# One VectorE instruction over real and imaginary part, for the rotations and the closing products of a convolution, in a transformer layer with experts

## The chip, the cores and the metric

The kernel runs on one core of a Trainium2 chip. The metric is device time of one execution in microseconds. The number given for a kernel is the median of its runs. Profiles come from one execution each. TensorE multiplies matrices, VectorE and ScalarE work on elements, GpSimd works on elements and issues indirect transfers, and SyncE issues the plain ones. In the rows of the profile they are PE, DVE, ACT, POOL and SP. Each engine takes its own instructions strictly in order and waits for the others at semaphores.

## What is computed

The input x has 8 batches of 1024 positions with 128 channels, in float32. The reference, cut to what matters:

```python
# block 1, on h = layernorm(x) without parameters
h = layernorm(h, gamma, beta)
conv = ifft(fft(filt) * fft(h))            # filt[t] = phazor**t * phazor_init
h = real(conv + last_conv * prog * phazor) # prog[t] = phazor**t
x1 = h + xn                                # xn = layernorm(x)
x = x + x1 + (silu(layernorm(x1) @ w1 + b1) @ w2 + b2)
# block 2: 8 experts, the best 2 of each token, weighted by a softmax over the two
x = x + moe(layernorm(x))
```

The kernel does the convolution without a Fourier transform, as a recurrence along the positions, for each of the 128 channels. With channels on the partitions, u (the normalized input, 128 x 1024) is multiplied by a complex table `in`. Real part `vr` and imaginary part `vi` are each scanned along the 1024 positions with a real decay. Then both are multiplied by a table `out`, and the result is the difference of the two products.

## The kernel before

Work is staged by batch. TensorE turns a batch's normalized rows so that channels lie on partitions (`hn_turn`), ScalarE copies the turned rows out as u (`conv_input`), VectorE does the convolution, TensorE turns it back (`conv_turn`), and VectorE adds it to xn (`x1_sum`, line 1189) and takes mean and variance (`moments`). GpSimd makes scale and shift out of these (`x1_scales`, lines 557 to 560), ScalarE normalizes with them (`x1_norm`, line 661), TensorE turns the rows (`h2_turn`), multiplies up (`mlp_up`) and down (`mlp_down`) with a SiLU of ScalarE between. VectorE adds the residual (`x2_sum`), the moments go through GpSimd and ScalarE again (`x2_scales`, `x2_norm`), and the rows are routed. For each batch VectorE chooses the pair of experts (`choose`) and computes each row's place (`positions`), and GpSimd scatters the batch's eight tiles of 128 rows to device memory by indirect transfers (`sort_rows`, line 584). When six batches are sorted, the experts begin on tiles of rows, which takes the last 200 us.

The input's own statistics run further ahead: VectorE's `x_statistics` and `x_moments`, then GpSimd's `x0_scales` (lines 546 to 551, with a power at line 549), then ScalarE's two normalizations (`x0_norm`, line 674, and `x0_plain_norm`, line 681).

The order on each engine is written out by hand. Round i handles several batches at once: on VectorE the residual sum of batch i - 1, `x1_sum` of i + 1, the choice of i - 2, the input's statistics of i + 4, the rotations of i + 2, the moments of i + 4, the positions of i - 2, and the scans, products and subtraction of i + 2. Batches 0 and 1 come before the rounds, and there the scans follow the rotations at once. On GpSimd a round does `x2_scales`, `x1_scales`, an accumulating transfer of x1 (`add_x1`), `x0_scales` of batch i + 3, and the eight scatters of batch i - 2.

All tensors of the convolution are slots of one buffer `work` of 128 x 18 x 1024 floats: in_re and in_im are slots 0 and 1, out_re and out_im slots 2 and 3, u is slot 6, vr and vi slots 7 and 8. For each of the eight batches VectorE runs seven instructions of 1024 columns: `vr = u * in_re` (line 1210), `vi = u * in_im` (1215), a scan of vr (1221) and of vi (1223), `vr = vr * out_re` (1224), `vi = vi * out_im` (1226) and `vi = vr - vi` (1231). An instruction that uses the result of the one in front of it waits for a semaphore that this one raises. `s_vo` orders VectorE's own work through `then` and `mark`; `s_ui` says that both rotations are done (ScalarE may write the next u), `s_vi` that vi is scanned, `s_ti` that vi is multiplied, `s_conv` that the convolution is ready.

Of the kernel before, what the change touches and what calls it, by code (L numbers as in the profile page):

```python
# [4 lines left out]
BATCHES, LENGTH, D = 8, 1024, 128  # L5
# [62 lines left out]
def block_moe_kernel(nc, x, cols, w1, w2, b2, router, mw1, mw2, out):  # L68
# [5 lines left out]
    ALU = mybir.AluOpType  # L74
# [7 lines left out]
    with ctx, nc.allow_low_precision(reason="counts of at most 64 are whole in bf16"):  # L82
        def sb(name, shape, dt=f32):
            return ctx.enter_context(nc.sbuf_tensor(name, shape, dt))

        def sem(name):
            return ctx.enter_context(nc.semaphore(name))
# [17 lines left out]
        work = sb("work", [128, 18, LENGTH])  # L105

        def slot(k):
            return work[:, k, :]

        def tiled(ap):  # L110
            return ap.rearrange("p (j d) -> p j d", d=D)

        in_re, in_im, out_re, out_im = slot(0), slot(1), slot(2), slot(3)
        hn, xn = tiled(slot(4)), tiled(slot(5))
        u, vr, vi = slot(6), slot(7), slot(8)
        x1, h2 = [tiled(slot(9)), tiled(slot(13))], tiled(slot(10))
# [16 lines left out]
        start_v = sb("start_v", [128, 4])  # L133
# [159 lines left out]
        s_vo = sem("vector_order")  # L293
# [6 lines left out]
        s_ui = sem("u_im_ready")  # L300
        s_vi = sem("v_im_ready")
        s_ti = sem("out_im_ready")
        s_conv = sem("conv_ready")
        s_t2 = sem("conv_turned")
# [49 lines left out]
        def after(eng, semaphore, count):  # L354

            if count > 0:
                eng.wait_ge(semaphore, count)
# [16 lines left out]
        def live(b):  # L374
            return 0 <= b <= LAST
# [740 lines left out]
        def _(v):  # L1116
            d = nc.vector
# [10 lines left out]
            def mark(ins):  # L1128

                ins.then_inc(s_vo, 1)  # L1130
                ordered[0] += 1
                return ordered[0]

            def then(ins):
                v.wait_ge(s_vo, mark(ins))
# [35 lines left out]
            def x2_sum(b):  # L1171
                v.wait_ge(s_dn, (b + 1) * FC)
                v.wait_ge(s_res[b], 16)
                if live(b - ROWBUFS):
                    v.wait_ge(s_sort[b - ROWBUFS], 16 * TPB)
                d.tensor_tensor(x2_of(b), tiled(down_p[:, :]), batch_of(resid, b), ALU.add).then_inc(s_x2, 1)

            def x2_stats(b):
                v.wait_ge(s_x2, b + 1)
                after(v, s_sc2, b)  # L1180
                moments(lambda j: x2_of(b)[:, j, :], stats2, mom2, s_x2m)
# [21 lines left out]
                after(v, s_sc0, b - 1)  # L1203
                aggregates(stats0, mom0[b % 2], s_x0m)

            def rotate_re(b):

                v.wait_ge(s_u, b + 1)
                after(v, s_conv, b)
                return mark(d.tensor_tensor(vr, u, in_re, ALU.mult))  # L1210

            def rotate_im(b):

                after(v, s_t2, b)
                d.tensor_tensor(vi, u, in_im, ALU.mult).then_inc(s_ui, 1)

            def scans(b, rotated):

                decay = decay_factor.to_broadcast([128, LENGTH])
                v.wait_ge(s_vo, rotated)  # L1220
                then(d.tensor_tensor_scan(vr, decay, vr, start_v[:, 0:1], ALU.mult, ALU.add))
                v.wait_ge(s_ui, b + 1)
                d.tensor_tensor_scan(vi, decay, vi, start_v[:, 1:2], ALU.mult, ALU.add).then_inc(s_vi, 1)
                then(d.tensor_tensor(vr, vr, out_re, ALU.mult))
                v.wait_ge(s_vi, b + 1)
                d.tensor_tensor(vi, vi, out_im, ALU.mult).then_inc(s_ti, 1)

            def convolution(b):

# [47 lines left out]
            def choose(b):  # L1277

                choose_first(b)
                choose_others(b)  # L1280
                choose_second(b)
                choose_pair(b)
                choose_places(b)
# [79 lines left out]
            def iteration(i):  # L1363


                b0, b1, b2, b4, chosen_b = i - 1, i + 1, i + 2, i + 4, i - 2
                if live(b0):
                    x2_sum(b0)
                if live(b0):
                    x2_stats(b0)  # L1370
                if live(b1):
                    x1_sum(b1)
                if live(chosen_b):
                    choose(chosen_b)
                if live(b4):
                    counted = x_statistics(b4)
                if live(b2):
                    rotated = rotate_re(b2)
                    rotate_im(b2)
                if live(b4):  # L1380
                    x_moments(b4, counted)
                if live(chosen_b):
                    positions(chosen_b)
                if live(b2):
                    scans(b2, rotated)
                if live(b2):
                    convolution(b2)

# [102 lines left out]
            tables(first_moments)  # L1491
            v.wait_ge(s_decay, 1)
            v.wait_ge(s_tab, 1)
            rotated = rotate_re(0)
            rotate_im(0)
            scans(0, rotated)
            convolution(0)
            weights()
            x1_sum(0)
            x_moments(2, x_statistics(2))  # L1500
            rotated = rotate_re(1)
            rotate_im(1)
            scans(1, rotated)
            convolution(1)
            x_moments(3, x_statistics(3))
            iteration(0)
# [121 lines left out]
```

## Time and profile before

| | us |
|---|---|
| median of 3 runs | 444.3 |
| lowest and highest run | 443.93, 446.59 |
| the profiled execution's own time | 446.09 |
| its span, first to last instruction | 444.3 |
| VectorE busy in the span | 349.3 (79%) |
| TensorE busy | 376.9 (85%) |
| ScalarE busy | 319.5 (72%) |
| GpSimd busy | 271.5 (61%) |

The profiled execution took 1.8 us more than its span, which lies around the instructions. In the rows of a timeline the first number is the start in us from the span's beginning and the second how long the instruction (or a run of like ones) lasted; a bracket behind it is the idle time of its engine in front of it and the instruction that ended it. An instruction's row can reach a little into the next one's, since it is counted until its last result is written; the distance from start to start is what it occupies of the engine.

### The profile page before, as it was taken

To read this page: it belongs to the slowest core of one execution; us is meant where nothing else is said; L and a number is where in the kernel's file an instruction comes from. 1 tells how busy PE (TensorE), PEld (TensorE's weight loads), DVE (VectorE), ACT (ScalarE), POOL (GpSimd) and SP (SyncE) were. 2 spreads that over 40 slices of the span, in tenths; PEclk is the share of its full clock that TensorE was granted. 3 is DMA by queue.
4 is the path that set the end of the run, shared out by engine and by line. 5 is a ranking of instruction groups with operands and counts; after the bars stand their busy time and mean duration, and the time that the engine had idled before them with its cause. 6 is when DMAs were issued, how large, how long until landed. Compare 5 with 4: busy or idle time off the path is not lost.

```text
span 444.3 us, 11234 instructions
## 1 busy us (share of the span) xinstructions
PE 376.9 (85%) x2723; PEld 321.1 (72%) x2723; DVE 349.3 (79%) x1332; ACT 319.5 (72%) x772; POOL 271.5 (61%) x339
## 2 busy tenths in 40 slices
PE   1173288797999999989979899999999999999970
PEld 1131257484867768666748899899999999999970
DVE  7999999798899989897652777887677777777770
ACT  4792586978889798689544786677777777777740
POOL 6890955645687798756483376477654555545451
PEclk9996589998989898999997999999999999999995
DMA  7649222110222221231323243444433333333200
GB/s 247 188 144 321 83 49 48 29 20 14 48 89 47 89 62 50 70 93 51 90 86 115 59 143 113 120 147 131 115 92 94 104 102 102 107 100 109 70 3 0
DMA packets 34434, 41.60 MB, mean 94 GB/s; under 512 B 5382, under 2 KB 29459, under 8 KB 34244
## 3 DMA queue, kind: packets, MB, share of 16 engines
q1 hardware_dynamic: 27236, 23.56, 18.4%
q0 software_dynamic: 7136, 17.33, 13.5%
q8 instruction: 25, 0.41, 0.4%
q14 instruction: 37, 0.30, 0.2%
HBM read 19.52 MB, written 18.92 MB: 86 GB/s over the span
## 4 chain that ended last, share of the span: by engine, by line
PE 55%; POOL 13%; DVE 11%; ACT 6%; issue 6%; POOLq 0%; DVEq 0%; ACTq 0%
PE up_p L1057 12%; PE down_p L1076 12%; PE down_p L876 8%; POOL sorted_rows L584 6%; PE turn_p L1057 5%; PE turn_p L1076 5%; PE up_p L865 5%; PE turn_p L853 3%; PE up_p L1066 2%; ACT work L674 2%; POOL scale L549 2%; PE route_p L918 2%; DVE stats L1158 1%; ACT rows L688 1%; ACT work L681 1%
## 5 line engine op out<-in xcount | busy, mean ns | idle before, releaser
L620 POOL DMA_INDIRECT out<-result,out_id x91 | 89.4, 983 | 68.1 <-DVE result L1564 47.2
L584 POOL DMA_INDIRECT sorted_rows<-rows,pos x64 | 71.8, 1122 | 37.6 <-issue 27.2
L865 PE MATMUL up_p<-h_t,work 128*128 128x512 f32 x128 | 67.7, 653 | 9.4 <-ACT work L648 8.1
L1057 PE MATMUL up_p<-xt,work 128*128 128x128 f32 x520 | 69.4, 277 | 0.6 <-ACT hid_t L806 0.5
L876 PEld LDWEIGHTS down_p<-w_sb,work 128*128 128x128 f32 x512 | 62.2, 196 | 9.9 <-issue 9.3
L1076 PE MATMUL down_p<-mw_sb,hid_t 128*128 x520 | 69.1, 276 | 0.1
L821 ACT ACTIVATE work<-mw_c 128x256 f32 x182 | 65.8, 416 | 0.3 <-issue 0.2
L876 PE MATMUL down_p<-w_sb,work 128*128 128x128 f32 x512 | 64.5, 281 | 0.1
L1057 PEld LDWEIGHTS up_p<-xt,work 128*128 128x128 f32 x520 | 63.2, 192 | 1.2 <-issue 1.1
L1076 PEld LDWEIGHTS down_p<-mw_sb,hid_t 128*128 128x128 f32 x520 | 63.3, 192 | 0.6 <-issue 0.5
L806 ACT ACTIVATE hid_t<-up_p 128x512 f32<-128x512 f32 x65 | 38.8, 597 | 29.8 <-PE up_p L1057 29.6
L853 PE MATMUL turn_p<-ident,work 128*128 128x128 f32 x192 | 29.9, 308 | 27.2 <-ACT work L674 11.4
L853 PEld LDWEIGHTS turn_p<-ident,work 128*128 128x128 f32 x192 | 25.6, 161 | 35.0 <-ACT work L674 11.5
L865 PEld LDWEIGHTS up_p<-h_t,work 128*128 128x128 f32 x128 | 23.8, 208 | 33.9 <-issue 19.0
L648 ACT ACTIVATE work<-up_p,b_all 128x512 f32<-128x512 f32 x64 | 40.5, 675 | 10.1 <-PE up_p L865 9.7
L1558 DVE SCALAR_TENSOR_TENSOR biased<-down_p,tin,biased 128x128 f32<-128x128 f32 x65 | 22.8, 350 | 23.6 <-PE down_p L1076 22.0
L1540 DVE SCALAR_TENSOR_TENSOR biased<-b_all,tin 128x128 f32<-128x128 f32 x91 | 32.0, 352 | 9.7 <-issue 9.7
L661 ACT ACTIVATE work<-work,shift,scale 128x128 f32<-128x128 f32 x64 | 25.5, 480 | 16.4 <-POOL shift L560 16.4
L1547 DVE SCALAR_TENSOR_TENSOR biased<-b_all,tin,biased 128x128 f32<-128x128 f32 x91 | 32.0, 352 | 3.6 <-issue 1.5
L801 ACT ACTIVATE xt<-up_p,one_col 128x128 f32<-128x128 f32 x91 | 33.0, 362 | 1.0 <-PE up_p L1066 1.0
L688 ACT ACTIVATE rows<-rows,shift,scale 128x128 f32<-128x128 f32 x64 | 25.5, 481 | 4.7 <-POOL shift L575 4.7
L549 POOL TENSOR_TENSOR scale<-var_eps,neg_half 128x16 f32<-128x16 f32 x8 | 27.2, 3405 | 0.7
(248 smaller groups left out, 744.2 us busy)
## 6 DMA issues: line engine op xcount, KB each, us to landing
tin<-sorted_rows SPq DMA_DIRECT2D x91, 136.0 KB, 2.2
resid<-in_x SPq DMA_DIRECT2D x8, 512.0 KB, 3.8
resid<-work POOLq DMA_DIRECT2D x8, 512.0 KB, 4.7
sorted_rows<-zeros SPq DMA_DIRECT2D x29, 136.0 KB, 2.4
out<-result,out_id POOLq DMA_INDIRECT x91, 2.3
work<-in_mw SPq DMA_DIRECT2D x1, 1024.0 KB, 6.3
sorted_rows<-rows,pos POOLq DMA_INDIRECT x64, 2.5
work<-in_w SPq DMA_DIRECT2D x1, 256.0 KB
```

The lines of the kernel that those rows point to most:

```text
L549: then(g.tensor_tensor(scale0[b % 2][:, :, :].rearrange("p a b -> p (a b)"), var_eps[:, :, :].rearrange("p a b -> p (a b)"), neg_half[:, : ...
L584: g.indirect_dma_start(sorted_dram, bass.IndirectOffsetOnAxis(pos[b % 2][:, j:j + 1], 0), rows[b % ROWBUFS][:, j, :], None).then_inc(s_sor ...
L620: g.indirect_dma_start(out_rows, bass.IndirectOffsetOnAxis(out_id[k][:, :], 0), result[k][:, :], None, bounds_check=TOKENS - 1, oob_is_err ...
L648: s_.activation(half(silu[c % 2], h), up_p[k % 3][:, :], ACT.Silu, bias=b1_all[:, c:c + 1])\
L801: s_.activation(xt[s % DEEP][:, :], xt_p, ACT.Identity, bias=one_col[:, :]).then_inc(s_xs, 1)
L806: s_.activation(hid_t[s % DEEP][:, :], mid_banks[bank_of(s)][:, :], ACT.Gelu).then_inc(s_gelu, 1)
L821: last = s_.activation(ring[s % RING][:, k * EF:(k + 1) * EF], mw1_c[:, bass.ds(at[k], EF)], ACT.Copy)
L853: last = t.transpose(turn_p[:, j * TILE:(j + 1) * TILE], src(j), ident[:, :])
L865: t.matmul(dst, w1_g[:, k], half(h_t, h), start=True, stop=True).then_inc(s_up, 1)
L876: last = t.matmul(down_p[:, j * D:(j + 1) * D], silu[c % 2][:, j * TILE:(j + 1) * TILE], w2_sb[:, c, :], start=False, stop=c == FC - 1, sk ...
L1057: last = t.matmul(mid_banks[bank_of(s)][:, c * TILE:(c + 1) * TILE], ring[s % RING][:, c * 128:(c + 1) * 128], xt[s % DEEP][:, :], start=T ...
L1076: last = t.matmul(y_banks[bank_of(s)][:, e * D:(e + 1) * D], hid_t[s % DEEP][:, c * 128:(c + 1) * 128], mw2_sb[:, bass.ds(at, D)], start=c ...
```

## The change

The two rotations become one instruction of 2 x 1024 columns. It reads u for both parts (the same 1024 columns twice), in_re with in_im, and writes vr with vi, which lie in neighbouring slots. The two products by `out` become one in the same manner. The scans stay two instructions, as does the subtraction. The order marks between the parts (`s_vo`) go: the first scan waits for `s_ui`, the fused product for `s_vi`. The fused rotation waits for the turned convolution of the batch before (`s_t2`) as a whole; only the imaginary part's rotation did so before.

```diff
+        both_in, both_out, both_v = work[:, 0:2, :], work[:, 2:4, :], work[:, 7:9, :]
...
-            def rotate_re(b):
+            def rotate(b):
 
                 v.wait_ge(s_u, b + 1)
                 after(v, s_conv, b)
-                return mark(d.tensor_tensor(vr, u, in_re, ALU.mult))
-
-            def rotate_im(b):
-
                 after(v, s_t2, b)
-                d.tensor_tensor(vi, u, in_im, ALU.mult).then_inc(s_ui, 1)
-
-            def scans(b, rotated):
+                d.tensor_tensor(both_v, u.unsqueeze(1).to_broadcast([128, 2, LENGTH]), both_in, ALU.mult).then_inc(s_ui, 1)
+
+            def scans(b):
 
                 decay = decay_factor.to_broadcast([128, LENGTH])
-                v.wait_ge(s_vo, rotated)
-                then(d.tensor_tensor_scan(vr, decay, vr, start_v[:, 0:1], ALU.mult, ALU.add))
                 v.wait_ge(s_ui, b + 1)
+                d.tensor_tensor_scan(vr, decay, vr, start_v[:, 0:1], ALU.mult, ALU.add)
                 d.tensor_tensor_scan(vi, decay, vi, start_v[:, 1:2], ALU.mult, ALU.add).then_inc(s_vi, 1)
-                then(d.tensor_tensor(vr, vr, out_re, ALU.mult))
                 v.wait_ge(s_vi, b + 1)
-                d.tensor_tensor(vi, vi, out_im, ALU.mult).then_inc(s_ti, 1)
+                d.tensor_tensor(both_v, both_v, both_out, ALU.mult).then_inc(s_ti, 1)
```

The calls follow: `rotate(b)` stands where `rotate_re(b)` and `rotate_im(b)` stood, and `scans(b)` takes no count.

VectorE's instructions around the rotations and scans of batch 2, before; `x0_scales`, `vector_order` and the like are semaphores, `work` is the buffer of all slots:

```order
L1210 TENSOR_TENSOR work<-work 128x1024 [waits conv_ready,u_ready]
L1215 TENSOR_TENSOR work<-work 128x1024 [waits conv_turned]
L1152 MEMSET spare_v 128x1 [waits x0_scales,vector_order]
L1164 BN_AGGR mom<-stats 128x2 x8
L1221 SCALAR_TENSOR_TENSOR work<-mag,start_v,work 128x1024 [waits vector_order]
L1223 SCALAR_TENSOR_TENSOR work<-mag,start_v,work 128x1024 [waits u_im_ready,vector_order]
L1224 TENSOR_TENSOR work<-work 128x1024
L1226 TENSOR_TENSOR work<-work 128x1024 [waits v_im_ready,vector_order]
L1231 TENSOR_TENSOR work<-work 128x1024 [waits out_im_ready]
```

The same place in the changed kernel, whose lines are numbered anew (1218 and 1219 are the scans, 1226 the subtraction):

```order
L1212 TENSOR_TENSOR work<-work 128x2048 [waits conv_turned,conv_ready,u_ready]
L1153 MEMSET spare_v 128x1 [waits x0_scales,vector_order]
L1165 BN_AGGR mom<-stats 128x2 x8
L1218 SCALAR_TENSOR_TENSOR work<-mag,start_v,work 128x1024 [waits u_im_ready]
L1219 SCALAR_TENSOR_TENSOR work<-mag,start_v,work 128x1024
L1221 TENSOR_TENSOR work<-work 128x2048 [waits v_im_ready]
L1226 TENSOR_TENSOR work<-work 128x1024 [waits out_im_ready]
```

Nothing changes places: seven instructions of 1024 columns become five, two of them with 2048. The wait between the two scans is gone, and the one in front of the products has moved ahead of both of them. The other engines' instructions are the same.

## Rows read from the trace of the kernel before

**Rows 1.** the chain that ended last, share of the span by engine (page, part 4)

```profile
PE 55%; POOL 13%; DVE 11%; ACT 6%; issue 6%; POOLq 0%; DVEq 0%; ACTq 0%
```

**Rows 2.** VectorE in order of time around batch 1: start us, us, engine, line

```profile
46.57 1.19 DVE L1210 TENSOR_TENSOR work<-work 128x1024 f32<-128x1024 f32 x1
47.68 1.23 DVE L1215 TENSOR_TENSOR work<-work 128x1024 f32<-128x1024 f32 x1
48.83 2.34 DVE L1221 TENSOR_TENSOR_SCAN work<-mag,start_v,work 128x1024 f32<-128x1024 f32 x1
51.20 2.36 DVE L1223 TENSOR_TENSOR_SCAN work<-mag,start_v,work 128x1024 f32<-128x1024 f32 x1
53.49 1.20 DVE L1224 TENSOR_TENSOR work<-work 128x1024 f32<-128x1024 f32 x1
54.72 1.23 DVE L1226 TENSOR_TENSOR work<-work 128x1024 f32<-128x1024 f32 x1
55.98 1.23 DVE L1231 TENSOR_TENSOR work<-work 128x1024 f32<-128x1024 f32 x1
```

**Rows 3.** groups by line: busy us, mean ns of one, idle before

```profile
L1246 DVE TENSOR_TENSOR first<-scored,pick 128x64 f32<-128x64 f32 x8 | 1.8, 225 | 0.3
```

**Rows 4.** GpSimd in order of time, the same stretch

```profile
44.50 0.20 POOL L557 TENSOR_TENSOR tmp<-mom,neg_one 128x8 f32<-128x8 f32 x1 [10.94 <-DVE mom L1164]
...
46.67 1.16 POOL L560 TENSOR_TENSOR shift<-tmp,scale 128x8 f32<-128x8 f32 x1
47.79 1.17 POOL L546 TENSOR_TENSOR var_eps<-mom,eps 128x8 f32<-128x8 f32 x1
48.93 2.24 POOL L547 TENSOR_TENSOR tmp<-mom,neg_one 128x8 f32<-128x8 f32 x1
51.23 0.20 POOL L548 TENSOR_SCALAR var_eps<-mom 128x8 f32<-128x8 f32 x1
51.51 4.75 POOL L549 TENSOR_TENSOR scale<-var_eps,neg_half 128x16 f32<-128x16 f32 x1
56.34 0.94 POOL L551 TENSOR_TENSOR shift<-tmp,scale 128x16 f32<-128x16 f32 x1
```

**Rows 5.** durations of two GpSimd lines: ns min/median/max, first to last start

```profile
L549 POOL TENSOR_TENSOR scale<-var_eps,neg_half x8: 2920/2936/4903, 14.1 to 163.8; 128x16 f32<-128x16 f32 x8
...
L584 POOL DMA_INDIRECT sorted_rows<-rows,pos x64: 956/965/3115, 117.8 to 294.7; - x64
```

**Rows 6.** ScalarE in order of time, the same stretch

```profile
47.86 3.18 ACT L661 ACTIVATE work<-work,shift,scale 128x128 f32<-128x128 f32 x8 [10.34 <-POOL shift L560]
...
57.31 3.19 ACT L674 ACTIVATE work<-resid,shift,scale 128x128 f32<-128x128 f32 x8
```

**Rows 7.** VectorE, then GpSimd, then ScalarE around batch 7's rotations

```profile
184.97 1.22 DVE L1210 TENSOR_TENSOR work<-work 128x1024 f32<-128x1024 f32 x1
186.11 1.22 DVE L1215 TENSOR_TENSOR work<-work 128x1024 f32<-128x1024 f32 x1
...
185.85 0.40 POOL L560 TENSOR_TENSOR shift<-tmp,scale 128x8 f32<-128x8 f32 x1
...
186.28 3.18 ACT L661 ACTIVATE work<-work,shift,scale 128x128 f32<-128x128 f32 x8 [3.24 <-POOL shift L560]
```

**Rows 8.** VectorE, then GpSimd, then ScalarE, batches 5 and 6

```profile
138.34 1.21 DVE L1210 TENSOR_TENSOR work<-work 128x1024 f32<-128x1024 f32 x1
...
147.81 1.22 DVE L1226 TENSOR_TENSOR work<-work 128x1024 f32<-128x1024 f32 x1
...
137.40 2.92 POOL L549 TENSOR_TENSOR scale<-var_eps,neg_half 128x16 f32<-128x16 f32 x1
...
145.50 1.93 POOL L584 DMA_INDIRECT sorted_rows<-rows,pos  x1 [0.30 <-issue]
147.73 0.96 POOL L584 DMA_INDIRECT sorted_rows<-rows,pos  x1 [0.30 <-issue]
...
159.78 3.19 ACT L661 ACTIVATE work<-work,shift,scale 128x128 f32<-128x128 f32 x8 [0.79 <-POOL shift L560]
```

More of the change, by code:

```diff
@@ L1377, in iteration @@
                 if live(b2):
-                    rotated = rotate_re(b2)
-                    rotate_im(b2)
+                    rotate(b2)
                 if live(b4):
@@ L1384, in iteration @@
                 if live(b2):
-                    scans(b2, rotated)
+                    scans(b2)
                 if live(b2):
@@ L1493, in _ @@
             v.wait_ge(s_tab, 1)
-            rotated = rotate_re(0)
-            rotate_im(0)
-            scans(0, rotated)
+            rotate(0)
+            scans(0)
             convolution(0)
@@ L1500, in _ @@
             x_moments(2, x_statistics(2))
-            rotated = rotate_re(1)
-            rotate_im(1)
-            scans(1, rotated)
+            rotate(1)
+            scans(1)
             convolution(1)
```

## The prediction

> **What bounds the kernel now.** I read the chain of waits that ended last first: TensorE holds 55% of it, GpSimd 13, VectorE 11, ScalarE 6 [rows 1]. All eight fused pairs lie in the first 200 of 444.3 us, where the chain passes from engine to engine, so I read that stretch in order of time, engine by engine. Around batch 1 VectorE never rests: rotation, rotation, scan, scan, product, product, subtraction start one behind the other from 46.57 to 55.98 us [rows 2]. Beside it GpSimd works out the scales of the next normalizations. Such an instruction of 8 columns takes 0.20 us when it meets no long VectorE instruction (44.50), but 1.16, 1.17 and 2.24 us at 46.67, 47.79 and 48.93, and each of these ends 0.12 to 0.15 us behind the start of the next VectorE instruction: 47.83 against 47.68, 48.96 against 48.83. The power at line 549 takes 4.75 us here and 2.92 at least [rows 2, 4, 5]. So a GpSimd instruction that begins while VectorE reads two SBUF operands lasts until that VectorE instruction is over. ScalarE waits for the outcome: 10.34 us for line 560, and its normalization at 57.31 starts 0.03 us behind the end of line 551 at 57.28 [rows 4, 6]. That wait, GpSimd behind VectorE and ScalarE behind GpSimd, is what the change touches.
>
> In the Trainium skill, "SBUF — State Buffer", section "Who interferes with whom", has this as a rule: a VectorE instruction with two SBUF inputs and a GpSimd instruction that reads SBUF exclude each other, and the later one stands still for the whole of the other. The stretched lines above agree with it. By that rule the two GpSimd terms below hold; without it only the VectorE gains would be left.
>
> **The change part by part.** *The fused instruction.* No row shows one of 2048 columns. Two products of the same kind: 64 columns take 0.225 us [rows 3], 1024 take 1.19 to 1.23 [rows 2], which is (1.21 - 0.225) / 960 = 1.03 ns a column; so 2048 take 1.21 + 1024 x 0.00103 = 2.26 us. From start to start an instruction that waits for nothing occupies 1.11 to 1.15 us (46.57 to 47.68, 47.68 to 48.83), and one whose successor needs its result 1.23 to 1.26 (53.49 to 54.72 to 55.98), some 0.1 more. The fused one then occupies 2.20, or 2.30 before a successor that needs it. From below the bound is 2 x (1.21 - 0.225) = 1.97 (nothing but columns), from above 2 x 1.26 = 2.52 (nothing saved). I take 2.20 and 2.30, the straight line through the rows.
>
> *VectorE, per batch.* The rotations took 2.26 together; 2.20 now where statistics stand between them and the scans (six batches), 2.30 where the scan follows at once (batches 0 and 1). From the first scan to the subtraction 7.15 us pass now (48.83 to 55.98): 2.37, 2.29, 1.23, 1.26. The wait between the scans goes (2.29 in place of 2.37), the second scan gets one before the fused product (2.37 for 2.29), and the pair costs 2.30 for 2.49: 6.96. So a batch gains 0.15 to 0.25 us, some 1.8 us of VectorE's time over eight batches. Most of it is not on the chain: VectorE waits for TensorE or ScalarE later in the same round. On the chain I count batch 0's, 0.1 us. The added wait for the turned convolution before the real part costs nothing: the residual sum that stands ahead of it on VectorE has waited for the same turn, and in batch 0 nothing is waited for.
>
> *Beside batch 1's rotations and products.* Line 560 (for batch 0's residual sum) starts 0.10 us behind the rotation (46.67, 46.57). Its end moves from 47.83 to 46.57 + 2.20 + 0.15 = 48.92, and ScalarE's normalization at 47.86 moves by 1.09 [rows 2, 4, 6]. Then line 546, line 547 and line 548 each need a turn. Before, they had the seams at 48.83 and 51.20, and the power began inside the second scan: 51.51, released when the product started at 53.49, and 2.77 us later, at 56.26, done. After, the seams are 48.87 (rotation to scan), 51.16 and 53.53 (scan to product). With the first one spent on line 560, at most line 546 slips through; line 547 stands behind the first scan and line 548 behind the second or on the seam. The power starts inside the fused product and is released at 53.53 + 2.20 = 55.73: done at 58.5, line 551 at 58.8 instead of 57.28. That is +1.5 for the normalization at 57.31. The least it can be is 0 (GpSimd finds a place at the middle of the fused instructions); 1.1 stands by line 560 alone.
>
> *Beside batch 7's rotations, line 560 again* (for batch 6's residual sum). It starts at 185.85 inside the first rotation (184.97), is done at 186.25, 0.14 behind the start of the second at 186.11, and ScalarE, which had waited 3.24 us, starts at 186.28 [rows 7]. The fused rotation starts 0.16 earlier by batch 6's shorter scans and products, and ends at 184.81 + 2.20 = 187.01: line 560 at 187.15, +0.9. Bounds: 0, and 1.1 without the earlier start. Beside the other batches' rotations line 560 was not held so long, and I count nothing there.
>
> *Sum.* -0.1 + 1.5 + 0.9 = +2.3 us. The profiled execution took 446.09 us (span 444.3), so it would take 448.4. The median before is 444.3, 1.8 below that execution; the same sum on it gives 446.6.
>
> **The rivals.** *GpSimd is not held longer, and the time falls.* Place: line 560 beside the rotations of batches 1 and 7. If a waiting read gets in between the two halves of the fused instruction, the port is free after some 1.1 us as before, and both GpSimd terms are 0. What is left are the gains on the chain: 0.1 in batch 0, 0.16 for scans and product of batch 4 and 0.07 for batch 5's rotation: -0.3, 444.0. If every gain of 1.8 counted it would be 442.5. It decides from the point where line 560 beside batch 1 lasts about 1.2 us and not 2.2. For it: no row shows an instruction of two halves. Against it: nothing in the rows shows a read let in before an instruction's end, and a scan of 2.34 us held line 547 for 2.24.
>
> *More is lost, in the sorting.* The row scatters of line 584 take 0.965 us in the median, but 1.93 at 145.50, behind a scan. The third, at 147.73, takes 0.96: it began 0.08 us before the second product of its batch (147.81), on the seam between the products [rows 5, 8]. That seam is gone, so a third scatter should stand behind the fused product, +1.0 us. For batch 4's scans this makes GpSimd later in front of batch 5: the power at 137.40 ran free, and would start at about 138.4, behind the rotation at 138.34 that now lasts until 140.4; it would end at 143.3 instead of 140.32, and after what GpSimd then waited for VectorE anyway about 2.0 us are left at the end of the next eight scatters. The scales behind them hold ScalarE at 159.78 (0.79 us of waiting). If all of it passes on: 2.3 + 2.0 = +4.3, 448.6. Against it: it is a race of some 0.1 us, and the next scan waits for TensorE, which gives GpSimd time to catch up. The same section of the Trainium skill says that descriptor generation should not be held by a product, as it needs the write side only; by that this rival would add nothing. The 1.93 and 3.1 us of line 584 under the scans speak against it.
>
> *The fused instruction does not run at one column per 1.03 ns,* with one operand read twice over. At 2.52 the rotation and the product of batch 1 and the rotation of batch 7 each hold GpSimd 0.3 longer: 446.6 + 0.9 = 447.5.
>
> **How the numbers follow.** Forecast, slower by about 2.3: 0.52, with its own range 445.2 (the 0.9 beside batch 7 alone) to 447.5 (the upper price of the instruction). Not held: 0.27, 442.5 to 444.8. More lost: 0.18. Slow instruction: 0.03. The range is 443.2 to 449.2: it leaves out the lower half of the second case and what the third may add beyond its sum. One per cent, 4.4 us, is about what a measurement of this kernel tells from no change. Slower by more takes the third case, nearly half of it (0.08), and 0.02 of the forecast's tail: 0.10. Faster by more than 4.4 is beyond all the gains of 1.8 together: 0.02. Within 1%: 0.88.
>
> **What would show it.** Right: fused instructions of about 2.26 us; line 560 beside batch 1's rotation over 2 us, and the normalization at 47.86 a microsecond later against that rotation; line 551 there after the subtraction's end; line 560 beside batch 7's rotation about 1.1 to 1.3 us; three of eight scatters stretched under batches 4 and 5 in place of two. Wrong: line 560 at 1.2 us or less, the normalizations at 57.31 and 186.28 no later, or an end that moves although they do not.

## The result and the profile after

The changed kernel takes 454.24 us in the median of 6 runs (451.92 to 458.29). Beside them the kernel before took 446.63 us (443.93 to 447.65, 6 runs). The ratio is 1.0179, with a 95% interval of 1.0125 to 1.0233: slower by 7.6 us, where I had forecast 2.3 and a range that ended at 449.2. The profiled execution took 452.99 us, with a span of 451.2.

In the profile the lines below the diff are numbered anew: the rotation is line 1212, the scans 1218 and 1219, the product 1221, the subtraction 1226. All lines of GpSimd and ScalarE are one higher: 561 is before's 560, 550 the power, 585 the scatters, 662 and 675 the normalizations.

The chain that ended last, by engine, answers to [rows 1]:

```profile
PE 57%; ACT 11%; POOL 10%; DVE 7%; issue 6%; DVEq 0%; POOLq 0%; ACTq 0%
```

ScalarE's share grew from 6 to 11%, and VectorE's, whose instructions became fewer, fell from 11 to 7. The chain now passes more often through ScalarE's normalizations; the shares alone do not show what they waited for, so the rows in order of time have to.

VectorE around batch 1, in order of time (start us, us), answers to [rows 2]:

```profile
46.21 2.26 DVE L1212 TENSOR_TENSOR work<-work 128x2048 f32<-128x2048 f32 x1
48.50 2.35 DVE L1218 TENSOR_TENSOR_SCAN work<-mag,start_v,work 128x1024 f32<-128x1024 f32 x1
50.77 2.33 DVE L1219 TENSOR_TENSOR_SCAN work<-mag,start_v,work 128x1024 f32<-128x1024 f32 x1
53.13 2.29 DVE L1221 TENSOR_TENSOR work<-work 128x2048 f32<-128x2048 f32 x1
55.46 1.23 DVE L1226 TENSOR_TENSOR work<-work 128x1024 f32<-128x1024 f32 x1
```

The fused instruction takes 2.26 to 2.29 us, as computed, and from the first instruction to the subtraction 9.25 us pass instead of 9.41. GpSimd in the same stretch, to [rows 4]:

```profile
46.31 2.22 POOL L561 TENSOR_TENSOR shift<-tmp,scale 128x8 f32<-128x8 f32 x1
48.49 0.19 POOL L547 TENSOR_TENSOR var_eps<-mom,eps 128x8 f32<-128x8 f32 x1
48.65 2.20 POOL L548 TENSOR_TENSOR tmp<-mom,neg_one 128x8 f32<-128x8 f32 x1
50.92 2.17 POOL L549 TENSOR_SCALAR var_eps<-mom 128x8 f32<-128x8 f32 x1
53.17 5.01 POOL L550 TENSOR_TENSOR scale<-var_eps,neg_half 128x16 f32<-128x16 f32 x1
58.26 0.22 POOL L552 TENSOR_TENSOR shift<-tmp,scale 128x16 f32<-128x16 f32 x1
```

Line 561 lasts 2.22 us for 1.16, to the end of the fused rotation. The next instruction slips through on the seam at 48.50, the two behind it stand one behind each scan, and the power is held by the fused product and done at 58.18. That is 11.97 us behind the start of the rotation, where the prediction had 11.93 (58.5 against 46.57). ScalarE's two normalizations, to [rows 6]:

```profile
48.56 3.18 ACT L662 ACTIVATE work<-work,shift,scale 128x128 f32<-128x128 f32 x8 [12.12 <-POOL shift L561]
...
58.51 3.19 ACT L675 ACTIVATE work<-resid,shift,scale 128x128 f32<-128x128 f32 x8 [0.61 <-POOL shift L552]
```

The second starts 1.2 us later than before (57.31). Counted from the start of the rotation, which itself came 0.36 earlier, the first is 1.06 us later than before and the second 1.56, as forecast (1.09 and 1.5). What the forecast did not count comes seventy microseconds later. The sorting of batch 0 beside batch 4's scans and products in the kernel before (GpSimd, then VectorE, then the normalization that follows on ScalarE):

```profile
121.06 1.92 POOL L584 DMA_INDIRECT sorted_rows<-rows,pos  x1 [0.30 <-issue]
123.28 0.96 POOL L584 DMA_INDIRECT sorted_rows<-rows,pos  x1 [0.30 <-issue]
...
123.34 1.22 DVE L1226 TENSOR_TENSOR work<-work 128x1024 f32<-128x1024 f32 x1
...
135.34 3.19 ACT L661 ACTIVATE work<-work,shift,scale 128x128 f32<-128x128 f32 x8 [0.41 <-POOL shift L560]
```

and in the changed kernel, with the two places further on where fused rotations meet GpSimd (batch 5's at 140.22, batch 6's at 162.94); this answers to [rows 8]:

```profile
123.13 1.78 POOL L585 DMA_INDIRECT sorted_rows<-rows,pos  x1 [0.30 <-issue]
125.21 2.06 POOL L585 DMA_INDIRECT sorted_rows<-rows,pos  x1 [0.30 <-issue]
...
140.41 4.87 POOL L550 TENSOR_TENSOR scale<-var_eps,neg_half 128x16 f32<-128x16 f32 x1
...
163.80 1.49 POOL L561 TENSOR_TENSOR shift<-tmp,scale 128x8 f32<-128x8 f32 x1
...
177.04 2.09 POOL L585 DMA_INDIRECT sorted_rows<-rows,pos  x1 [0.30 <-issue]
...
204.28 2.08 POOL L585 DMA_INDIRECT sorted_rows<-rows,pos  x1 [0.30 <-issue]
...
124.16 2.29 DVE L1221 TENSOR_TENSOR work<-work 128x2048 f32<-128x2048 f32 x1
126.48 1.22 DVE L1226 TENSOR_TENSOR work<-work 128x1024 f32<-128x1024 f32 x1
...
140.22 2.27 DVE L1212 TENSOR_TENSOR work<-work 128x2048 f32<-128x2048 f32 x1
...
162.94 2.29 DVE L1212 TENSOR_TENSOR work<-work 128x2048 f32<-128x2048 f32 x1
...
138.38 3.18 ACT L662 ACTIVATE work<-work,shift,scale 128x128 f32<-128x128 f32 x8 [1.37 <-POOL shift L561]
...
165.32 3.18 ACT L662 ACTIVATE work<-work,shift,scale 128x128 f32<-128x128 f32 x8 [2.80 <-POOL shift L561]
```

The third scatter, which used the seam between the two products (123.28 against 123.34), now begins inside the fused one and lasts to 127.27, 0.79 us beyond the start of the subtraction at 126.48: 2.06 us for 0.96. So are the third scatters of batches 2 and 3, at 177.04 (2.09) and 204.28 (2.08), which took 0.96 and 0.97 before. Then the power begins 0.19 us behind batch 5's fused rotation and takes 4.87 us for 2.92. Line 561 in front of batch 5's normalization takes 1.49 us for 0.20. ScalarE's waits for line 561 grow with it: 0.41 to 1.37, 0.79 to 2.80.

The Trainium skill, "SBUF — State Buffer", section "Who interferes with whom", infers that descriptor generation is not held by such a product, as it needs the write side. Here the scatter beside the fused product took 2.06 us and its five successors 0.96, so for these indirect transfers the measurement decides otherwise.

Beside batch 7's rotation nothing was held, against the forecast [rows 7]:

```profile
189.99 0.20 POOL L561 TENSOR_TENSOR shift<-tmp,scale 128x8 f32<-128x8 f32 x1
...
190.50 2.29 DVE L1212 TENSOR_TENSOR work<-work 128x2048 f32<-128x2048 f32 x1
```

GpSimd, late by some 4 us, now comes 0.5 us before the rotation there and no longer inside it. The ranges of the two lines of [rows 5] and of line 561 (ns min/median/max) sum up who is held: the power's median rises from 2936 to 3432, the scatters' stays, and the longest of line 561 takes 2223 where line 560 had 1157.

```profile
L550 POOL TENSOR_TENSOR scale<-var_eps,neg_half x8: 2921/3432/5009, 13.8 to 167.0; 128x16 f32<-128x16 f32 x8
...
L585 POOL DMA_INDIRECT sorted_rows<-rows,pos x64: 956/965/2981, 119.9 to 301.2; - x64
...
L561 POOL TENSOR_TENSOR shift<-tmp,scale x8: 201/202/2223, 46.3 to 217.3; 128x8 f32<-128x8 f32 x8
```

### The profile page after: what moved, and what is told of

Read it like the earlier page. It is cut to its first block, busy times and chain, and to the rows that moved or that the text cites. A ratio compares the mean times of both kernels' runs of the same rounds, so it can differ in the third digit from the quotient of the medians.

```text
span 451.2 us, 11202 instructions
## 1 busy us (share of the span) xinstructions
PE 377.5 (84%) x2723; PEld 322.0 (71%) x2723; DVE 347.7 (77%) x1316; ACT 319.3 (71%) x772; POOL 288.1 (64%) x339
## 4 chain that ended last, share of the span: by engine, by line
PE 57%; ACT 11%; POOL 10%; DVE 7%; issue 6%; DVEq 0%; POOLq 0%; ACTq 0%
PE up_p L1058 12%; PE down_p L1077 12%; PE down_p L877 9%; POOL sorted_rows L585 6%; PE turn_p L1058 5%; PE up_p L866 5%; PE turn_p L1077 5%; PE turn_p L854 4%; ACT work L662 3%; ACT work L675 3%; ACT work L682 2%; PE up_p L1067 2%; ACT rows L689 2%; ACT work L649 1%; PE route_p L919 1%
## 5 line engine op out<-in xcount | busy, mean ns | idle before, releaser
L585 POOL DMA_INDIRECT sorted_rows<-rows,pos x64 | 76.7, 1198 | 41.0 <-issue 23.2
L866 PE MATMUL up_p<-h_t,work 128*128 128x512 f32 x128 | 65.4, 632 | 16.3 <-ACT work L649 15.1
L877 PEld LDWEIGHTS down_p<-w_sb,work 128*128 128x128 f32 x512 | 63.8, 200 | 10.5 <-issue 9.9
L877 PE MATMUL down_p<-w_sb,work 128*128 128x128 f32 x512 | 66.3, 286 | 0.1
L550 POOL TENSOR_TENSOR scale<-var_eps,neg_half 128x16 f32<-128x16 f32 x8 | 30.5, 3811 | 0.7
```

The lines of the kernel that those rows point to most:

```text
L585: g.indirect_dma_start(sorted_dram, bass.IndirectOffsetOnAxis(pos[b % 2][:, j:j + 1], 0), rows[b % ROWBUFS][:, j, :], None).then_inc(s_sor ...
L866: t.matmul(dst, w1_g[:, k], half(h_t, h), start=True, stop=True).then_inc(s_up, 1)
L877: last = t.matmul(down_p[:, j * D:(j + 1) * D], silu[c % 2][:, j * TILE:(j + 1) * TILE], w2_sb[:, c, :], start=False, stop=c == FC - 1, sk ...
```

## The experiments

Ratios are against the kernel before, run beside them. Two theories stood against each other at first. *Length*: an instruction twice as long holds GpSimd twice as long. *Seams*: what was lost are the waits and places between instructions that the change also removed or moved.

**The change in parts.** Four kernels: the rotations fused alone (second scan and products as before, their own waits kept); the products fused alone; both fused over the parts, but over 512 columns at a time, so that there are as many instructions as before; and nothing fused with the changed kernel's waits.

```diff
# e2_product_only, against the changed kernel
-                d.tensor_tensor(both_v, u.unsqueeze(1).to_broadcast([128, 2, LENGTH]), both_in, ALU.mult).then_inc(s_ui, 1)
+                d.tensor_tensor(vr, u, in_re, ALU.mult)
+                d.tensor_tensor(vi, u, in_im, ALU.mult).then_inc(s_ui, 1)
# e4_waits_only: the same, and
-                d.tensor_tensor(both_v, both_v, both_out, ALU.mult).then_inc(s_ti, 1)
+                d.tensor_tensor(vr, vr, out_re, ALU.mult)
+                d.tensor_tensor(vi, vi, out_im, ALU.mult).then_inc(s_ti, 1)
# e1_rotation_only, against the changed kernel
-                d.tensor_tensor_scan(vr, decay, vr, start_v[:, 0:1], ALU.mult, ALU.add)
+                then(d.tensor_tensor_scan(vr, decay, vr, start_v[:, 0:1], ALU.mult, ALU.add))
...
+                then(d.tensor_tensor(vr, vr, out_re, ALU.mult))
                 v.wait_ge(s_vi, b + 1)
-                d.tensor_tensor(both_v, both_v, both_out, ALU.mult).then_inc(s_ti, 1)
+                d.tensor_tensor(vi, vi, out_im, ALU.mult).then_inc(s_ti, 1)
# e3_halves_of_columns, against the changed kernel (the rotation in the same way)
-                d.tensor_tensor(both_v, both_v, both_out, ALU.mult).then_inc(s_ti, 1)
+                for h in range(2):
+                    last = d.tensor_tensor(halves(both_v, h), halves(both_v, h), halves(both_out, h), ALU.mult)
+                last.then_inc(s_ti, 1)
```

e1, rotations alone:

> Only the two rotations are one instruction; scans and products with their waits are those of before. Length theory (GpSimd's reads are held for as long as the VectorE instruction with two SBUF operands lasts, and 2.29 us holds longer than 1.2): line 560 beside batches 1, 2 and 6 stays held (1.5 to 2.2 us each), the third scatter of each batch is free again (0.96 us); about 449 to 451 us against 446.6 before and 454.2 changed. Seam theory (the loss comes from the waits that went, which left gaps for GpSimd): the scans and products have their waits, so about the time of before, 446 to 448.

Measured: 448.53 us, ratio 1.0059 (1.002 to 1.0099): a small loss, just below what *length* expected and just above *seams*.

e2, products alone:

> Only the two products are one instruction, and the scans follow each other without a wait; the rotations are two. Length theory: line 560 of batch 1 lasts 1.2 us as before, the third scatter of batches 4 to 7 is held (about 2 us), the power in front of batch 5's scatters races with the rotation; 448 to 451 us. If it is the rotation alone that costs: 446 to 447.

Measured: 453.22 us, ratio 1.0143 (1.0057 to 1.0229), more than was expected.

e3, both in halves of the columns:

> Both parts in one instruction, but of 2 x 512 columns, two of them for the rotation and two for the product: as many instructions of 1024 columns as before, with the operand shapes and the waits of the changed kernel. Length theory: no GpSimd instruction is held over 1.2 us by them, line 560 beside batch 1 lasts about 1.2 us; 445 to 448 us. Rival (the form of the operands, u read twice, or the waits that went are what costs): 452 to 455.

Measured: 446.31 us, ratio 0.9995 (0.9951 to 1.004), as *length* expected.

e4, the waits alone:

> Nothing is fused; only the waits are those of the changed kernel (no wait between the scans or between the products). Length theory: line 560 as before, VectorE 0.1 to 0.2 us per batch shorter; the third scatter can lose the gap between the products, which costs up to 1.1 us a batch; 445 to 449 us. Seam theory: most of the loss, 451 to 455.

Measured: 446.57 us, ratio 1.0001 (0.9963 to 1.0039), as *length* expected.

The same columns and operands, paired in the same way, cost nothing when each instruction stays at 1.2 us, and the waits cost nothing either. The length is the cause. The products weigh more than the rotations (1.4% and 0.6%), though the forecast had most of its loss at a place where both meet GpSimd. The third scatter shows what the product's length does: it takes 2.07 us beside the fused product and 1.00 beside the halves. GpSimd of e2, then of e3:

```profile
124.31 2.07 POOL L585 DMA_INDIRECT sorted_rows<-rows,pos  x1 [0.30 <-issue]
```

```profile
124.04 1.00 POOL L585 DMA_INDIRECT sorted_rows<-rows,pos  x1 [0.30 <-issue]
```

**Out of the rotation's way.** In e5 the changed kernel's rotation waits until the scales of the batch before are made, so that it cannot hold line 561. In e6 the product is in halves besides, as in e3.

```diff
                 after(v, s_t2, b)
+                after(v, s_sc1, b)
```

> The changed kernel, and the fused rotation waits until GpSimd has the scale and shift of x1 of the batch before (line 560 of the kernel before). Length theory: line 560 lasts 0.20 us beside every batch, ScalarE's normalizations of x1 beside batches 1, 2 and 6 are no longer late by it, VectorE gives up to 1 us of its own waiting; what the product costs stays: 450 to 453 us. If the rotation cost nothing beyond the product: 454 as the changed kernel.

Measured: 452.01 us, ratio 1.0147 (1.0075 to 1.0219). Line 561 takes 0.20 us everywhere, and 1.5% stay.

> As e5_wait_for_scales, and the product over both parts comes in two instructions of 2 x 512 columns. Length theory: both held reads are gone, the third scatter of a batch lasts about 1 us: 444 to 447 us, at or a little below the kernel before. Rival (more than held reads is lost): 449 or more.

Measured: 448.1 us, ratio 1.001 (0.9959 to 1.0061): the time lies between the two expectations, the ratio is not separable from 1. With the product halved, what is left of the change costs nothing that can be measured: a fused rotation behind line 561 is free, and the 1.5% of e5 are the product's.

**Shorter still.** If length costs, shorter scans should gain. e7 is e3 with each scan in two of 512 columns, the second one starting from the last column of the first.

```diff
-                d.tensor_tensor_scan(vr, decay, vr, start_v[:, 0:1], ALU.mult, ALU.add)
-                d.tensor_tensor_scan(vi, decay, vi, start_v[:, 1:2], ALU.mult, ALU.add).then_inc(s_vi, 1)
-                v.wait_ge(s_vi, b + 1)
+                for h in range(2):
+                    for k, part_of in ((0, vr), (1, vi)):
+                        first = start_v[:, k:k + 1] if h == 0 else part_of[:, HALF - 1:HALF]
...
+                v.wait_ge(s_vi, 4 * b + 4)
```

> As e3_halves_of_columns, and the two scans in halves of 512 columns too, the second half of each going on from the last column of the first: no VectorE instruction of the convolution is over about 1.3 us. Length theory carried on: the first two scatters of a batch last about 1.9 and 1.0 us instead of 2.9 and 1.9, the power at line 549 less than 4.2; VectorE pays 0.1 to 0.4 us a batch; 441 to 445 us, below both kernels. Rival (the held reads of the scans are not on the path): 446 to 449.

Measured: 448.63 us, ratio 1.0044 (1.0004 to 1.0084): slower, where a gain was expected. The held instructions did become shorter, the first scatter of batch 0 from 2.91 to 1.84 us and two powers from 4.75 and 4.90 to 3.79 and 3.83. Others became longer: a third power went from 2.92 to 3.98, the third scatter of batch 2 from 0.96 to 1.96, and the scans take 2.45 and 2.43 us a pair of halves, for 2.34 in one. That the time follows from these is argued; no run takes them apart.

**TensorE's clock.** In the changed profile the granted clock is at the lower level (1.2 of 2.4 GHz) for most of two stretches of rounds 4 and 5, behind waits of TensorE of 2.64 and 2.33 us for ScalarE (us, busy times of the engines, clock as a share of full speed, DMA share, GB/s; before has 1.00 in both). Over the whole profile the mean is not lower, 0.949 against 0.942 before.

```profile
158.00:166.00 8.00, 7.63 (x29) 6.10 (x30) 6.74 (x28) 4.04 (x7) 7.58 (x11) 0.58 0.10 35
186.00:193.00 7.00, 7.00 (x28) 5.59 (x27) 6.34 (x26) 5.36 (x12) 4.95 (x7) 0.54 0.21 50
```

e8 is the changed kernel with eight unused matmuls in those waits.

```diff
+                    if b in (4, 5) and c == 1 and h == 1:
+                        pe.wait_ge(s_x2, b)
+                        for _ in range(8):
+                            t.matmul(down_p[:, 0:128], ones_f[:, :], mean_f[:, :], start=True, stop=True)
                     after(pe, s_silu, n - 2)
```

> The changed kernel with eight matmuls of 128 columns, whose result is not used, in the two waits of TensorE (2.64 and 2.33 us) behind which it ran at half clock in rounds 4 and 5. If the half clock is part of the loss: granted clock near 1.0 from 158 to 166 and from 186 to 193 us of the span, eight matmul pairs of the down projection in 2.0 us and not 3.8, and the time 2 to 4 us below the changed kernel, 450 to 452. If it is beside the path: 453 to 455.

Measured: 454.55 us, ratio 1.0206 (1.0131 to 1.0281). The clock stayed at full in both stretches, and fell elsewhere:

```profile
80.00:105.00 25.00, 22.01 (x121) 16.78 (x119) 18.87 (x59) 19.28 (x42) 12.69 (x14) 0.86 0.11 22
158.00:166.00 8.00, 7.14 (x43) 5.15 (x42) 7.47 (x37) 5.00 (x9) 7.06 (x11) 1.00 0.16 54
186.00:193.00 7.00, 6.14 (x33) 4.18 (x33) 6.51 (x29) 6.74 (x14) 4.69 (x7) 1.00 0.21 42
225.00:240.00 15.00, 15.00 (x80) 11.32 (x79) 8.68 (x45) 4.38 (x9) 10.42 (x13) 0.84 0.24 85
```

Keeping the clock full at these two places gave none of the 2 to 4 us. That does not put the clock off the path. In the changed kernel's chain the down projection (line 877) of the first stretch takes twice as long as the next one, start and us:

```profile
162.42 3.71 PE down_p L877 x16
...
167.91 1.78 PE down_p L877 x16
```

Where e8 gained by this and lost it again is shown behind the table below.

**Which batches.** e9, e10 and e12 keep the rotations apart, with the changed kernel's waits, and fuse the products in batches 4 to 7 (scatters run beside them), in 0 to 3 (none do), and in 4 and 5.

```diff
+                if b >= 4:
+                    d.tensor_tensor(both_v, both_v, both_out, ALU.mult).then_inc(s_ti, 1)
+                else:
+                    d.tensor_tensor(vr, vr, out_re, ALU.mult)
+                    d.tensor_tensor(vi, vi, out_im, ALU.mult).then_inc(s_ti, 1)
# e10: if b < 4, e12: if b in (4, 5)
```

> Separate rotations with the changed kernel's waits; the two products are fused in batches 4 to 7 only, where row scatters run beside them. Theory that the loss comes from the scatters (third scatter held by the fused product, GpSimd late for the next scales): most of what the fused products cost everywhere comes back, 450.5 to 454 against a kernel before at 446.5; third scatter of the first batch sorted about 2.06 us, line 560's instruction beside batch 2 about 0.5. Rival, the prediction's own place (the scales beside batch 1, before any scatter): under 1 us is lost, 446 to 448.

Measured: 452.73 us, ratio 1.0156 (1.0087 to 1.0226), as the theory of the scatters expected.

> The same with the products fused in batches 0 to 3 only, where no row scatter runs. Theory of the scatters: 445.5 to 447.5, third scatters 0.96 us. Rival, the scales of the early batches (power 4.9 us beside batch 1, then 3.9 at 74.5 beside batch 2): 450 to 453, and the normalizations of x1 later by a microsecond or more from the third one on.

Measured: 448.86 us beside 447.8 for the kernel before, ratio 1.0019 (0.9978 to 1.0061). By the ratio nothing measurable is lost.

> Separate rotations with the changed kernel's waits; the products are fused in batches 4 and 5 only (fused in 4 to 7 they cost 1.56%). If the loss is a sum of single delays, here it is that of one third scatter (+1.1 us) and of the power behind it (+0.9 us): ratio 1.003 to 1.007, third scatter of the first sorted batch about 2.06 us, of the three others about 0.96. If instead only the last rounds before the experts count (what comes earlier is made up again while other engines wait): ratio 0.997 to 1.002. If the first delay sets all that follows late: 1.010 or more.

Measured: 451.57 us, ratio 1.0089 (1.0052 to 1.0126), between two of the expectations: more than the sum of the delays that the rows show. In its profile they are one third scatter (2.07 for 0.96 us) and one power (3.80 for 2.92). The rows do not explain the 0.89%, as the table below shows.

The place is settled by e9 and e10: what the products measurably cost, they cost beside the scatters. The size is not: some 2 us of held instructions in e12 beside 4.0 us of time.

**The delay by itself.** e13 and e14 take the kernel before, with nothing fused, and let GpSimd's fourth scatter wait until the subtraction beside it is done; e13 does so for batches 0, 2 and 3, e14 for batch 0.

```diff
                 for j in tiles:
+                    if b in (0, 2, 3) and j == 3:
+                        pool.wait_ge(s_conv, b + 5)
                     g.indirect_dma_start(sorted_dram, bass.IndirectOffsetOnAxis(pos[b % 2][:, j:j + 1], 0),
```

> The kernel before, nothing fused; GpSimd's fourth scatter of batches 0, 2 and 3 waits until VectorE's subtraction beside it is done, which starts it some 1.3 us later than before (third scatters stay at 0.96 us). Theory that a late GpSimd is the whole cause and that its lateness costs more than itself: 5 to 9 us, ratio 1.011 to 1.020, as the fused products of batches 4 to 7 cost. If each delay passes on one to one: three times 1.3 and up to 1.0 at a power, ratio 1.006 to 1.011. If the fused product does something else besides: under 1.005.

Measured: 454.06 us, ratio 1.0184 (1.014 to 1.0229), as the first theory expected.

> The same wait for batch 0's fourth scatter only. One to one: 1.3 us, and up to 1.0 at the power behind it, ratio 1.003 to 1.006. If the lateness costs more than itself, as in the kernel with fused products in batches 4 and 5: 1.006 to 1.012. If something else in the fused product costs the time: 0.998 to 1.002.

Measured: 453.2 us, ratio 1.0167 (1.0125 to 1.0209), above every expectation. GpSimd, then ScalarE, of e14:

```profile
127.70 0.96 POOL L586 DMA_INDIRECT sorted_rows<-rows,pos  x1 [1.86 <-DVE work L1233]
...
139.69 1.52 POOL L547 TENSOR_TENSOR tmp<-mom,neg_one 128x8 f32<-128x8 f32 x1
141.29 1.07 POOL L548 TENSOR_SCALAR var_eps<-mom 128x8 f32<-128x8 f32 x1
142.44 2.92 POOL L549 TENSOR_TENSOR scale<-var_eps,neg_half 128x16 f32<-128x16 f32 x1
...
138.57 3.19 ACT L663 ACTIVATE work<-work,shift,scale 128x128 f32<-128x128 f32 x8 [2.03 <-POOL shift L560]
```

One wait lets GpSimd stand 1.86 us instead of 0.30, 1.56 more, at one place of the kernel before, and the kernel loses 1.67%, some 7 us (5.6 to 9.3 by the interval), about what the change loses. What two more such waits add, the runs do not separate from nothing. A late GpSimd is enough for a loss of this size; a fused product need do nothing else.

How it grows can be followed when each profile is counted from its own first `placed` (VectorE's instruction that computes the rows' places, line 1288 before, 1283 after), which puts aside what differs earlier in an execution. Times are in us behind it:

| | before | waits only (e4) | changed | changed, waits filled (e8) | products of 4, 5 (e12) | one delay (e14) |
|---|---|---|---|---|---|---|
| `placed` of batch 0 in the profile | 116.67 | 118.22 | 118.74 | 120.39 | 121.28 | 118.26 |
| batch 0 sorted, GpSimd goes on | 13.92 | 13.83 | 14.88 | 14.87 | 14.89 | 15.48 |
| ScalarE's `x1_norm` behind it | 18.67 | 18.57 | 19.64 | 19.64 | 19.65 | 20.31 |
| first scatter of batch 1 | 25.63 | 25.52 | 27.52 | 27.52 | 27.61 | 27.97 |
| the next `x1_norm` | 43.11 | 42.92 | 46.58 | 46.59 | 45.63 | 45.99 |
| `placed` of batch 2 | 48.10 | 48.10 | 51.84 | 48.65 | 48.66 | 52.50 |
| the experts' first upward product | 131.36 | 131.75 | 136.26 | 136.33 | 132.52 | 136.24 |
| mean granted clock in between | 0.94 | 0.95 | 0.95 | 0.96 | 0.97 | 0.92 |

From that product on all six take about the same time to the end of their spans (195.8 to 196.4 us). Against the kernel with the waits alone, the changed one is 1.05 late when batch 0 is sorted, which is the held third scatter, 2.0 at the next scatters, which adds the held power, 3.7 at the next normalization, in front of which line 561 is held, and 4.5 when the experts begin. e14 goes the same way.

Behind the next scatters two things mix. One is collisions: GpSimd's instructions, now later, come to lie inside the next rotations and are held again (lines 547 and 548 in e14, the power in the changed kernel), and ScalarE waits 1.4 to 2.8 us where it waited 0.4 to 0.8. The other is TensorE's clock. Up to the next `x1_norm` e8 is as late as the changed kernel, with the same held instructions, but TensorE had the full clock from 158 to 166 us, and `placed` of batch 2 comes 0.55 us late in e8 and 3.74 late in the changed kernel. At `x2_norm` of batch 5 (213.36 us of its span) e8 is 1.3 us late; then it meets the lower level twice, and at the experts it is as late as the changed kernel again:

```profile
223.00:230.00 7.00, 7.00 (x36) 7.00 (x36) 3.71 (x17) 1.47 (x2) 5.36 (x6) 0.51 0.25 90
243.50:247.00 3.50, 3.50 (x19) 3.50 (x18) 0.00 (x0) 2.84 (x7) 2.59 (x4) 0.51 0.29 100
```

In e10 no third scatter is held in the sorting of batches 0 to 3 (0.96 to 1.02 us), and `x1_norm` behind batch 0 comes at 18.58, as in e4. Its first scatter of batch 1 still comes 2.9 us later than e4's, with the lower level ahead of it:

```profile
134.00:142.00 8.00, 8.00 (x30) 5.97 (x29) 7.55 (x33) 5.36 (x12) 7.21 (x12) 0.57 0.35 68
```

So rows of single profiles, in which these stretches lie at different places, do not price the collisions.

e12 makes the same point from the other side. Behind its first `placed` it is 0.8 us late at the experts: one third scatter and one power did not grow in this profile, which had the highest clock of the six. Its span is 4.3 us longer than e4's all the same, and 3.1 of that lie ahead of the first `placed`, where it runs e4's instructions, at a mean clock of 0.87 against 0.90. Of e14's 6.4 us beside the kernel before, 1.6 lie ahead in this way, and 4.9 between `placed` and the experts. What makes the start differ no run shows.

**Does anything beat both?** e11 is the kernel before with e5's wait in front of the real part's rotation.

> The kernel before with one wait more: the real part's rotation waits for the scales of x1 of the batch before, so that line 560's instruction is never held. If the 1.16 us that it lasts beside batch 1 cost the kernel before anything, 444.5 to 446 against 446.5; if later waits swallow it or the rotation's delay eats it, 446 to 448. Does it beat both kernels: I give it one chance in four.

Measured: 446.9 us beside 447.8, ratio 0.9992 (0.9944 to 1.0041). No kernel of the study was measurably faster than the one before.

## Why the prediction was wrong

The direction held, and so did the mechanism, a GpSimd instruction that lasts as long as the fused one beside it. The place of the loss and its size did not. By the prediction's own steps:

- *The reading of the rows*: of the three instructions said to end 0.12 to 0.15 us behind the start of VectorE's next one, the third (48.93 + 2.24 = 51.17) ends 0.03 ahead of it (51.20). That it lasts as long as the scan is not touched by this.
- *The fused instruction*, 2.26 us by a straight line: 2.26 to 2.29 in sixteen of them. Right.
- *VectorE, per batch*, a gain of 0.15 to 0.25 us: 9.25 for 9.41 us around batch 1. Right; that it is off the chain fits e4, where the shorter waits alone left the ratio at 1.0001.
- *Beside batch 1's rotations and products*, +1.5: the rows came as described, and against the rotation the normalization moved by 1.56. But in the time little of it is seen: fused products in batches 0 to 3 cost 0.2%, not separable from nothing, and fused rotations everywhere 0.6%. What takes it up before the first scatter the runs do not show.
- *Beside batch 7's rotations*, +0.9: did not come. Line 561 came 0.5 us ahead of the rotation and took 0.20 us. Rows of before cannot say which instruction lies inside a rotation 140 us later, once GpSimd is 4 us late.
- *"Beside the other batches' rotations line 560 was not held so long, and I count nothing there"*, and nothing for the products beside the scatters. This step failed. The third scatter was held in three batches of four (2.06 to 2.09 us for 0.96), the power beside batches 3 and 5 (4.96 and 4.87 for 2.92), line 561 beside batches 2 and 6 (1.63 for 0.51, 1.49 for 0.20). Not each of these costs: line 561 beside batch 2 takes 1.62 in e4 too, whose time is that of before. Fused products in batches 4 to 7 alone, beside the scatters, cost 1.56%, and in batches 0 to 3 nothing measurable.
- *The rival "More is lost, in the sorting"* named this mechanism, with its place and its race, and got 0.18. Its working was right as far as it went: 1.0 us at the scatter and 2.0 at the end of the next eight; the rows have 1.05, and 2.0 at the first of the next eight. It stopped there; by the experts the rows have 4.5, to which later collisions, two more third scatters and the places of TensorE's lower clock contribute in shares that stay open. Its objection, "the next scan waits for TensorE, which gives GpSimd time to catch up", was the error behind the chance: 1.56 us of delay at that place (e14) cost 1.67%, though e12's profile made up for most of a held scatter and a held power by the experts. The slack was in the row of ScalarE's normalization behind the sorting, 0.41 us of waiting for GpSimd: GpSimd was already the last to arrive.
- *The rivals "not held" and "a slow instruction"* fell with the first row.

Of the 7.6 us between 446.6 and 454.24, 2.3 are the level of the kernel before, whose median in these runs was 446.63 instead of 444.3; the other 5.3 are what the sum lacked.

What stays open is how some 2 us of delay become 4 to 8. One delay of 1.56 us cost 1.67%, three cost 1.84%, and fused products in batches 4 and 5 cost 0.89% for about 2 us of held instructions, of which its profile shows 0.8 behind them. The steps are not proportional. That fits a chain of races, and it fits a shift in where TensorE's clock falls; no run took the two apart.

## What to carry to other kernels

Fewer, longer instructions on VectorE are dear when GpSimd reads SBUF beside them: each seam between two instructions is a place where GpSimd gets in, and what is saved in start-up (0.2 us a batch here) is small against a seam lost on the path. The same columns in instructions of 1.2 us cost nothing (e3). Before fusing, look in the trace for GpSimd instructions that end just behind the start of a VectorE instruction, and count them in every round, scatters included. Where an engine's waiting for GpSimd is only some tenths of a microsecond, price a delay there by putting one in by hand, and not by its own length: here a wait of one and a half microseconds cost seven. Before a difference between two profiles is put down to such a delay, compare the granted clock of the same stretches.

The Trainium skill, "VectorE: DVE Perf Modes", section "Rules for kernel authors", advises for chained VectorE operations not to fuse for performance, and to keep the number of operations small. For VectorE alone this case agrees with the smaller number, by 0.16 us around batch 1; for the kernel it does not, by 1.79%.

## What I had not expected of the hardware

The issue of an indirect transfer is held as arithmetic is. A scatter takes 0.96 us alone, 2.06 when it begins inside the fused product, and 2.91 when it begins 0.4 us into a scan. In both cases it ends 0.8 to 0.95 us behind the end of that VectorE instruction (127.27 against 126.45, 122.83 against 121.88), about the time that it takes alone.

A GpSimd instruction with a single tensor operand is held just as long: line 549 took 2.17 us beside a scan, and 0.19 elsewhere.

TensorE's mean granted clock is 0.96 at most in every run, and the stretches at the lower level lie at different places in most of the profiles. Runs of the kernel before took 443.34 us at a mean granted clock of 0.956 and 449.7 at 0.931, so two single executions can differ by more than the effect of one edit.
